# One activation over two PSUM banks and shared features in a per-pixel MLP, and a transpose mode for delta times u

## The reference, cut to what matters

```python
# layer 0
u = silu(causal_conv(xin)); delta = softplus(dt @ W_dt.T + b_dt)
h = exp(delta * A) * h + (delta * u) * B          # scan over the pixels, 256 channels x 16 states
y = (sum_n h * C + u * D) * silu(z); x = x + y @ W_out.T
# layer 1: f has 64, 32 and then 16 channels per pixel
f = lrelu(conv1x1(gn(x), sw1, sb1)); f = lrelu(conv1x1(f, sw2, sb2)); f = conv1x1(f, sw3, sb3)
feat = concat([f broadcast over 128 depth points, pts])        # 17 channels
h = lrelu(mw1 @ feat + mb1); h = lrelu(mw2 @ h + mb2); h = lrelu(mw3 @ h + mb3)
x = x + sigmoid(mw4 @ h + mb4)                    # one value per depth point and pixel
```

## Time and profile before

| | us |
|---|---|
| median of three runs | 9535.09 |
| profiled execution, its time | 9542.0 |
| its span | 9540.2 |
| layer 0, first to last product | about 5990 |
| layer 1 | about 3545 |

### The profile page before, as it was taken

One profiled execution on the slowest core, in us unless ns is written; L12 is line 12 of the kernel. 1 busy time (PEld: TensorE's weight loads), 2 busy tenths in 40 slices (PEclk: granted clock), 3 DMA queues, 4 the chain that ended last, 5 costly groups with the idle time before them and its releaser, 6 DMA issues. The chain is left out here.

```text
span 9540.2 us, 453563 instructions
## 1 busy us (share of the span) xinstructions
PE 9231.1 (97%) x201032; PEld 3923.3 (41%) x201032; DVE 8877.5 (93%) x10176; ACT 8419.0 (88%) x14729; POOL 5791.6 (61%) x2582
## 2 busy tenths in 40 slices
PE   7999999999999999999999999999999999999999
PEld 4555555555555555555555555222222222222222
DVE  6999999999999999999999999899999999999998
ACT  6888878888888888887888887899999999999999
POOL 6999999999999999999999999000000000000000
PEclk9999999999999999999999999999999999999999
DMA  4333333333333333333333333000000000000000
GB/s 116 92 95 92 86 80 90 92 95 90 88 83 84 97 94 97 85 84 81 82 85 87 84 84 78 21 22 22 20 22 22 21 21 22 22 20 22 22 20 19
DMA packets 375653, 605.58 MB, mean 63 GB/s; under 512 B 95808, under 2 KB 96434, under 8 KB 373186
## 3 DMA queue, kind: packets, MB, share of 16 engines
q1 hardware_dynamic: 370752, 574.99, 23.1%
q10 hardware_dynamic: 2338, 0.95, 0.0%
q0 software_dynamic: 608, 0.62, 0.0%
HBM read 236.45 MB, written 71.30 MB: 32 GB/s over the span
## 5 line engine op out<-in xcount | busy, mean ns | idle before, releaser
L1055 DVE TENSOR_TENSOR_SCAN arena<-arena,carried,ps 128x512 f32<-128x512 f32 x3968 | 4754.2, 1259 | 332.2 <-PE ps L478 320.4
L902 POOL TENSOR_TENSOR arena<-arena 128x1024 f32<-128x1024 f32 x2048 | 4792.6, 2377 | 131.9 <-PE ps L489 77.6
L1119 DVE SCALAR_TENSOR_TENSOR arena<-arena,neg_p 128x512 f32<-128x512 f32 x4096 | 2755.5, 745 | 0.1
L769 ACT ACTIVATE arena<-arena,a_neg 128x512 f32<-128x512 f32 x4096 | 2662.6, 710 | 13.2 <-DVE arena L1055 6.1
L478 PE MATMUL ps<-arena 64*32 64x128 f32 x131072 | 2322.5, 276 | 46.5 <-DVE arena L1055 34.8
L841 ACT ACTIVATE arena<-ps,b2t 128x512 f32<-128x512 f32 x3840 | 2330.9, 698 | 41.1 <-PE ps L604 12.7
L478 PEld LDWEIGHTS ps<-arena 64*32 64x32 f32 x131072 | 1847.4, 106 | 1170.4 <-DVE arena L1055 663.9
L604 PE MATMUL ps<-arena,w2s 32*32 32x512 f32 x32768 | 1566.5, 601 | 34.0 <-ACT arena L841 29.5
L848 ACT ACTIVATE arena<-ps,bm 128x1024 f32<-128x1024 f32 x1024 | 1163.7, 1136 | 2.1 <-PE ps L615 2.1
L615 PE MATMUL ps<-arena,m 64*32 64x512 f32 x16384 | 1120.4, 600 | 4.0 <-ACT arena L848 1.2
L489 PE MATMUL ps<-arena,sel 128*32 128x512 f32 x8192 | 1012.5, 613 | 23.1 <-DVE arena L1066 11.5
(11 more groups left out here) (137 smaller groups left out, 6437.6 us busy)
## 6 DMA issues: line engine op xcount, KB each, us to landing
arena<-arena SPq DMA_DIRECT2D x4096, 64.0 KB, 2.4
arena<-c_d SPq DMA_DIRECT2D x1024, 128.0 KB, 3.2
xr<-in_x SPq DMA_DIRECT2D x128, 256.0 KB, 3.6
x_d<-xr SPq DMA_DIRECT2D x128, 256.0 KB, 3.4
xr<-x_d SPq DMA_DIRECT2D x128, 256.0 KB, 2.9
out<-arena SPq DMA_DIRECT2D x128, 256.0 KB, 2.1
xs<-in_x SPq DMA_DIRECT2D x96, 256.0 KB, 3.9
arena<-in_x SPq DMA_DIRECT2D x4, 2048.0 KB, 18.5
```

The lines of the kernel that those rows point to most:

```text
L769: A(dA[(UNITS * t + m) % DR][:, gi, :], drep[:, e, :], ACT.Exp, scale=a_neg[:, e, 2 * gp + gi:2 * gp + gi + 1]).then_inc(s_dA, 1)
L902: nc.gpsimd.tensor_tensor(hc[m % CR], H[:, m % HR, :, :], crep[:, 2 * gp:2 * gp + 2, :], ALU.mult).then_inc(s_ch, 1)
L1055: V.tensor_tensor_scan(H[:, m % HR, gi, :], dA[(UNITS * t + m) % DR][:, gi, :], dbu[m % 2].rearrange("p (l g) -> p g l", g=2)[:, gi, :], 0 ...
L1119: m = V.scalar_tensor_tensor(out=t1[k % 4][:, q, :], in0=g[par], scalar=neg_p[:, i:i + 1], in1=gs_[par], op0=ALU.max, op1=ALU.add)
```

## The change

**Layer 1's chunk.** A chunk is now 32 depth points x 2048 pixels in place of 128 x 512: four chunks (`depth` = n % 4) share the features of 2048 pixels. A tile holds 4 blocks of 512 pixels (N/4 apart) x 32 channels; all partitions of a tile have the same depth point, and `neg_p` and `b2t` are laid out to match. PE's `mm2` keeps its code. Each of its halves (two banks) now holds tiles whose bias is one and the same column, so ACT's `leaky2` reads the half with one 128x1024 activation; in the shared steps the second half is one 128x512 activation beside DVE's bank.

**Features.** They are made once in four chunks, for 2048 pixels: two first products of two column tiles each (k = 0 of depth 0 and 1), one second product of two tiles with a block-diagonal `sw2` (k = 0 of depth 2), one third product 128x128 with a block-diagonal matrix (k = 4 of depth 2), `spread_g` at k = 5 of depth 3. Their ACT steps are 128x512, three in four chunks. Their input comes by four loads of its own in four chunks, from `x1_d` into the four `xs` tiles. The loads of x1 for the sum and the stores of the result go through `wide`: (32 depth points, 4 blocks) on the partitions, 2 KB in each, as before.

**Layer 0.** `transpose_du` calls `nc.tensor.transpose` in place of the matmul with the identity, eight times as before.

```diff
+        def wide(v, n):
+            b, i, depth = n // T, n % T // 4, n % 4
+            return v[b, 32 * depth:32 * depth + 32, :].rearrange("d (j s) -> (d j) s", j=4)[:, i * L:(i + 1) * L]
...
-                sp.dma_start(xr[place], x1_d[n // T, :, n % T * L:(n % T + 1) * L]).then_inc(s_x[place], 16)
+                sp.dma_start(xr[place], wide(x1_d, n)).then_inc(s_x[place], 16)
+            def load_features(s, pair):
+                if s > 1:
+                    sp.wait_ge(s_f1, 2 * (s - 1) + pair + 1)
+                b, i = (s - 1) // (T // 4), (s - 1) % (T // 4)
+                for j in (2 * pair, 2 * pair + 1):
+                    first = j * (N // 4) + i * L
+                    sp.dma_start(xs[j], x1_d[b, :, first:first + L]).then_inc(s_xs[j], 16)
...
-                        m = mm(pp[:, c // 2, (c % 2 * 2 + h) * P:(c % 2 * 2 + h + 1) * P], du[:, h, c, :], idn[:, :], start=True, stop=True)
+                        m = nc.tensor.transpose(pp[:, c // 2, (c % 2 * 2 + h) * P:(c % 2 * 2 + h + 1) * P], du[:, h, c, :], idn[:, :])
...
+            def first_layer(s, pair):
...
+                for a in range(2):
+                    tile, _ = feature_tile(s, 2 * pair + a)
+                    m = mm(f_ps[64 * a:64 * a + 64], s1r[:, (s - 1) // (T // 4), :], tile, start=True, stop=True)
+                m.then_inc(s_f1, 1)
...
-            def leaky2(t, k, half):
+            def leaky2(t, n, k, half):
                 act.wait_ge(s_m2, t * (2 * NG) + (2 * k + half + 1))
                 if half == 0:
-
                     act.wait_ge(s_m3, t * NG + (k - 3))
-                for j in (2 * half, 2 * half + 1)[:1 if half == 1 and k in SHARED else 2]:
-                    a = A(t2[k % 4][:, j, :], m2_ps[:, j, :], ACT.Prelu, bias=b2t[:, GQ * k + j:GQ * k + j + 1], alpha=SLOPE)
-                a.then_inc(s_t2, 1)
+                last, bias = 3 if half == 1 and k in SHARED else 2 * half + 2, NG * (n % 4) + k
+                A(t2[k % 4][:, 2 * half:last, :], m2_ps[:, 2 * half:last, :], ACT.Prelu, bias=b2t[:, bias:bias + 1], alpha=SLOPE).then_inc(s_t2, 1)
...
-                    if k == 5 and ahead:
-                        spread_g(t + 1, 1 - par)
+                    if k == 5 and ahead and i % 4 == 3:
+                        spread_g(i // 4 + 2, (i // 4 + 1) % 2)
```

More of the change, by code:

```diff
@@ L155, in mamba_sdf_kernel @@
         gs_ = [over(42 + i, 1) for i in range(2)]
[L156 to L159, removed]
+        f1 = [over(44 + i, 1) for i in range(2)]
+        f2 = over(46, 1)
+        sg = over(47, 1)
+        ob = [over(48 + i, 1) for i in range(2)]
         ps = ctx.enter_context(nc.psum_tensor("ps", [P, 8, L], F32))
@@ L349, in _ @@
             sp.wait_ge(s_st1, NT + 1)
+            sp.wait_ge(s_st, NT)
+            for pair in range(2):
+                load_features(1, pair)
             for n in range(4):
                 load_x1(n)
+            for pair in range(2):
+                load_features(2, pair)
             for n in range(NT):
@@ L576, in first_body, with second_layer, third_layer @@
                         conv(t + 2, 1, h, a)
[L578 to L593, removed]
+            def first_layer(s, pair):
+                for j in (2 * pair, 2 * pair + 1):
+                    tile, loaded = feature_tile(s, j)
+                    pe.wait_ge(s_xs[j], loaded)
+                if pair == 0:
+                    pe.wait_ge(s_g, s)
+                else:
+                    pe.wait_ge(s_f1l, 2 * s + 1)
+                for a in range(2):
+                    tile, _ = feature_tile(s, 2 * pair + a)
+                    m = mm(f_ps[64 * a:64 * a + 64], s1r[:, (s - 1) // (T // 4), :], tile, start=True, stop=True)
+                m.then_inc(s_f1, 1)
+            def second_layer(s):
+                pe.wait_ge(s_f1l, 2 * s + 2)
+                for a in range(2):
+                    m = mm(f_ps[64 * a:64 * a + 64], s2[:, :], f1[a], start=True, stop=True)
+                m.then_inc(s_f2, 1)
+            def third_layer(s):
+                pe.wait_ge(s_f2l, s + 1)
+                mm(f_ps, gw[:, :], f2, start=True, stop=True).then_inc(s_gp, 1)
             def mm2(t, k):
@@ L629, in layer1 @@
             def layer1(n):
-                t, first, ahead = n + 1, n == 0, real(n + 1)
-                f_a, f_b, f_c = features(t + 1, n + 1)
+                t, first, ahead = n + 1, n == 0, n // 4 + 1 < NT // 4
+                s, depth = n // 4 + 2, n % 4
                 for k in range(NG):
@@ L820, in first_body, with first_layer, second_layer @@
                 diagonals(t + 1)
[L822 to L833, removed]
-            def leaky2(t, k, half):
+            def first_layer(s, pair):
+                b = (s - 1) // (T // 4)
+                act.wait_ge(s_f1, 2 * s + pair + 1)
+                act.wait_ge(s_f2, s)
+                A(f1[pair], f_ps, ACT.Prelu, bias=b1r[:, b:b + 1], alpha=SLOPE).then_inc(s_f1l, 1)
+            def second_layer(s):
+                act.wait_ge(s_f2, s + 1)
+                act.wait_ge(s_gp, s)
+                A(f2, f_ps, ACT.Prelu, bias=bs2[:, :], alpha=SLOPE).then_inc(s_f2l, 1)
+            def leaky2(t, n, k, half):
                 act.wait_ge(s_m2, t * (2 * NG) + (2 * k + half + 1))
@@ L855, in layer1 @@
             def layer1(n):
-                t, first, ahead = n + 1, n == 0, real(n + 1)
-                f_a, f_b = features(t + 1, n + 1)
+                t, first, ahead = n + 1, n == 0, n // 4 + 1 < NT // 4
+                s, depth = n // 4 + 2, n % 4
                 for k in range(NG):
@@ L1201 @@
         mw3_bd[32 * j:32 * j + 32, 16 * (j % 2):16 * (j % 2) + 16] = mw3.T
-    for k in range(4):
-        for j in range(8):
-            mw4_bd[16 * j:16 * j + 16, k, 8 * k + j] = mw4[0]
+    for v in range(4):
+        for j in range(4):
+            for e in range(2):
+                r = 32 * j + 16 * e
+                mw4_bd[r:r + 16, v, 4 * (2 * v + e) + j] = mw4[0]
     eye = np.eye(P, dtype=f)
```

124 lines of the change are left out of this document (69 added, 55 removed).

## The result

| | before | after |
|---|---|---|
| median of four runs, us | 9534.48 | 9327.4 |
| lowest and highest | 9533.27 to 9541.98 | 9321.45 to 9330.18 |
| ratio to before, with its 95% interval | 1 | 0.978 (0.9763 to 0.9797) |
| profiled execution: time, span | 9542.0, 9540.2 | 9327.85, 9326.0 |

The change makes the kernel 2.2% faster: 207 us between the medians, 214 between the two profiled executions. The prediction was right, with 9320 for the median and 9327 for the profiled execution.

What follows compares the result with a forecast made beforehand. It took a chain of PE and ACT working in turn to bound layer 1, with POOL busiest in layer 0. 9542.0 - 169 (layer 1) - 50 (layer 0) + 4 (between) = 9327 profiled, 9320 median; range 9190 to 9440.

Steps and rivals of the forecast that it cites:

- The chain sets the pair of steps: Layer 1: PE and ACT work in turn in a closed chain; a pair of steps falls from 6.79 to 6.50 us.
- The wide activation: Layer 1, ACT: two 128x1024 activations take 2.13 us in place of 2.42 for four 128x512; layer 1 gains 169 us.
- ACT's own sum: Layer 1, pair after k = 0: ACT's work totals 6.71 us, 0.21 over 6.50, in three depths.
- Features, DVE's copies and the DMAs at nothing: Layer 1: fewer feature products and DVE copies, and four new loads in four chunks, change the time by nothing.
- Between the layers: Once, before g is ready: a second first product, its activation and two more loads ahead cost 4 us.
- Transposes: Layer 0, PE: eight instructions in place of sixteen, about 1.06 us for 2.05; PE gains 1.0 in a chunk.
- The 50 us: Layer 0's gain from PE's earlier transposes, taken as 50 us within bounds of 0 to 112.
- POOL's waits for PE: Layer 0, a sign of being right: these waits, 77.6 us in 96 before, would be halved.
- DVE as the pace: Rival 1, layer 1: the chain loosens and DVE's 24.9 us sets the chunk; about 9159 us, chance 0.10.
- DVE's bank late: Rival 2, layer 1 shared steps: PE waits for DVE's bank, chunk 27.66 us; about 9512 us, chance 0.06.
- The clock did not fall behind the transposes: Rival 3, layer 0: transposes lower PE's granted clock in every chunk, +198 us; 9568 us, chance 0.05.
- the transpose mode would have no effect: Rival 4, layer 0: transposes remain the same sixteen instructions; 9370 us, chance 0.05.

Runs made afterwards that it cites:

- `SHARED = (0, 4)`: The changed kernel with the two banks that DVE reads in k = 0 and 4 in place of 1 and 3: 9269.77 us, ratio 0.9723.

## Why the prediction was right, point by point

- **The chain sets the pair of steps.** Right. It closes in the kernel after by the same five terms (1.20 + 2.12 + 0.05 + 1.10 + 2.02 = 6.49), and moving one product onto it (+1.01 in the pair) or taking 30 us of DVE and 33 of PE in 1000 off beside it (no change) bears it out.
- **The wide activation.** 2.13 was taken for 2.42, the trace has 2.12; a pair of 6.50, and the trace has 6.48. By the figures of the Trainium skill, "ScalarE: Activation LUTs", section "What ACT_TABLE_LOAD costs", a pair would have gained 0.38 where 0.31 were measured; the choice for the rows was right. ACT's own sum was taken as 6.71 and is 6.70. The lengthening in its pair was taken as 0.21 and is 0.27 (0.22 for the late start, 0.05 for two slower activations). The chunk of 26.16 is 26.13, so 169 us was slightly low: 174.7 in the profiled executions, 167 by the run with this part alone.
- **Features, DVE's copies and the DMAs at nothing.** Right, and shown by the layout without the wide activation: 0.03 in a chunk, 4 us. It was closer than the prediction says: a pair with a feature product is 6.32 of PE's own work, 0.16 under the chain's 6.48, and the prediction did not work out this margin. DVE came to 95.4%, 24.9 of 26.13, as its sum said.
- **Between the layers.** +4 forecast, +3.9 measured, in the parts that it named: about 0.9 for the loads, and 2.89 for the second product and its activation.
- **Transposes.** One instruction each, as supposed, and the eight that were to take about 1.06 take 1.10. The Trainium skill, "TensorE: Matmul & The Clock Gate", section "Terms", would have given 0.5; the trace does not agree. The 50 us, a choice between 0 and 112, is 43.4 in the profiled pair and 51 with this part alone. POOL's waits for PE were to halve: 77.6 to 35.4, and these 42.2 are nearly the 43.4. DVE's longest wait before a scan in the 1.5 to 5 us behind the start of the transposes has a median of 0.21 over the 128 chunks, and had 1.16: PE's earlier end reaches DVE, as the prediction had it.
- **How firm layer 0's number is.** The kernel with wide activations alone left layer 0 as it was, and still ended it 16.5 us before the kernel before did (5976.39 against 5992.90). The clock differs between these two: the trace of before has TensorE at 0.50 for 167 us until then, the other for 140. So a single pair of traces gives layer 0's gain no closer than some 17 us. All the traces together do better: in the ten with the transpose mode the group norm's first product starts at 5934.68 to 5952.47, mean 5943.3, in the two without it at 5977.46 and 5993.97, mean 5985.7. That is 42 us, and 41.5 in the pair with the same 167 us at 0.50. The size is shown; that it came so near to the 50 is luck, since it was chosen between 0 and 112. So is 214 measured where 215 was forecast: layer 1 gave 6 more than its term, layer 0 7 less.
- **The rivals.** DVE as the pace (9159) did not come, since the chain did not loosen. DVE's bank late did not come in this kernel; it is real at `SHARED = (0, 4)`. The clock did not fall behind the transposes: 1.00 in both windows, and one stretch at 0.50 within 10 us behind the 128 groups. What the Trainium skill says in "TensorE: Matmul & The Clock Gate", section "Part 4: PE-mode transpose", cost nothing here with dense products around 1.1 us of transposes. That the transpose mode would have no effect is refuted by the eight instructions.

What the prediction did not ask is what else lay in the chain. It treated the shared steps as given. They stood in the odd steps, outside the chain, and moving them to k = 0 and 4 was worth 47 us (57 with the sigmoid moved as well). What the bank at k = 1 is worth where it stands, by ACT's own sum in that pair, was not measured: no run leaves it out of the kernel after.

## What to carry to other kernels

When two engines both read 99%, follow one period through the timeline and write it as a closed sum; only what stands in the sum pays, and the same 1.01 us product costs all or nothing depending on which side of the wait it is issued. It costs nothing only as long as it fits into the wait: when the chain becomes shorter once more it begins to cost (0.27 of its 1.01 at `SHARED = (0, 4)`). Where the busiest engine is held up by many short waits, what a shorter neighbour gives is about the waits that vanish (42 us of POOL's here, for 43 us of time), not its own length times its count (128 x 1.0). When one engine can take work off another, as DVE takes two banks off ACT here, choose the work that stands in the chain; and expect less than its full length, since the next limit (PE's own work, ACT's own sum) may lie close behind.

## What the runs showed of the hardware that was not expected

- A transpose of a 128x128 fp32 block is one instruction where the product with the identity is two, and takes half the time: 1.10 against 2.05 for eight. It leaves no mark in the granted clock: one stretch at 0.50 begins within 10 us behind the 128 groups, and layer 0 has fewer of them than before (28 for 33).
- The same two wide activations last 2.12 in most pairs and 2.17 in the pair that starts late (8019.87 above). Why was not tried.
- Layer 0 ended 17 us apart in two executions with the same instructions in it (167 and 140 us at 0.50 of the clock), while layer 1, at 1.00 nearly throughout, repeats to a few hundredths in each chunk. The times of whole runs go with it: of the 21 runs of the kernel before in the three sets, the twelve with a mean granted clock of 0.990 took 9534 to 9549 us, the four with 0.992 took 9525 to 9531.
